# Two steps of a head group multiplied with the values as one job, and the planner's costs and due times rewritten

## The reference: one transformer block over 16 sequences

```python
mod = (silu(c) @ wmod).reshape(16, 6, 1, 256)           # sa, ca, ga, sb, cb, gb per sequence
ga, gb = (sign-keeping maximum of |g| and 0.25)
h = layernorm(x) * (1 + ca) + sa
Q, K, V = (h @ w.T + b), split into 16 heads of 16
scores = Q @ K^T / 4 + slope[head] * (k - q), causal    # [16, 16, 1024, 1024]
x = x + ga * (softmax(scores) @ V @ o_w.T + o_b)
h = layernorm(x) * (1 + cb) + sb
x = x + gb * ffn(h)          # silu(gate) * up, down; width 704; inputs and weights rounded
                             # to a 4-bit grid with one scale per 16 numbers (fp4_linear)
```

## Time and profile before

| what | before |
|---|---|
| median of 3 runs | 3672.09 us (3669.64 to 3675.01) |
| the profiled execution's own time | 3680.17 us |
| its span, first to last instruction | 3678.4 us |
| PE busy | 3400.2 us (92%) |
| DVE busy | 2859.7 us (78%) |
| ACT busy | 1862.1 us (51%) |
| POOL busy | 1082.0 us (29%) |
| granted TensorE clock, mean | 0.944 |

### The profile page before, as it was taken

The page is one execution under the profiler, slowest core; times in us unless marked ns, Lnnn a source line. Parts: engine busy times, 40 slices in busy tenths (PEclk is TensorE's granted clock), DMA queues, the critical chain, the costliest instruction groups (busy, mean ns, idle before and its releaser), DMA issues.

```text
span 3678.4 us, 62613 instructions
## 1 busy us (share of the span) xinstructions
PE 3400.2 (92%) x24952; PEld 1950.1 (53%) x24952; DVE 2859.7 (78%) x4538; ACT 1862.1 (51%) x2475; POOL 1082.0 (29%) x794
## 2 busy tenths in 40 slices
PE   6889999999999999999999999999999999999887
PEld 3345555555555555555555555555555555555455
DVE  7877869778786987868788786987868789687665
ACT  1555455555554555455555554655455555555441
POOL 2112324223242322324133142232323223241233
PEclk7889999999999999999998999999998999999898
DMA  8251413314323332423314323332423314332010
GB/s 152 55 81 28 76 40 68 65 28 77 56 53 60 52 70 39 79 44 61 65 32 72 56 50 63 51 68 42 79 48 56 66 33 71 57 50 54 16 32 12
DMA packets 134929, 207.65 MB, mean 56 GB/s; under 512 B 38848, under 2 KB 98832, under 8 KB 134640
## 3 DMA queue, kind: packets, MB, share of 16 engines
q1 hardware_dynamic: 134640, 203.66, 31.3%
HBM read 63.65 MB, written 17.89 MB: 22 GB/s over the span
## 4 chain that ended last, share of the span: by engine, by line
PE 71%; DVE 14%; ACT 10%; issue 2%; POOL 1%; DMA 1%; SPq 1%; ACTq 0%; POOLq 0%; DVEq 0%
PE banks L783 12%; PE banks L919 9%; PE banks L767 9%; ACT arena L982 8%; DVE top L1218 8%; PE banks L802 8%; PE banks L896 8%; PE banks L903 7%; PE banks L826 5%; PE banks L912 3%; PE banks L857 3%; PE banks L877 3%; PE banks L748 3%; ACT L982 2%; PE banks L887 1%
## 5 line engine op out<-in xcount | busy, mean ns | idle before, releaser
L1218 DVE TENSOR_REDUCE top<-banks 128x2 f32<-128x1024 f32 (+3 forms) x1280 | 1371.8, 1114 | 274.7 <-PE banks L748 171.4
L982 ACT ACTIVATE arena<-banks 128x1024 f32<-128x1024 f32 (+2 forms) x1280 | 1160.7, 940 | 784.4 <-PE banks L748 520.3
L802 PE MATMUL banks<-ka,qa 58*128 58x512 f32 (+3 forms) x3072 | 625.3, 442 | 130.1 <-ACT arena L982 94.2
L767 PE MATMUL banks<-qa,ka 60*128 60x512 f32 (+3 forms) x3072 | 590.9, 424 | 79.7 <-ACT arena L982 46.7
L783 PE MATMUL banks<-arena,va 128*17 128x512 f32 (+3 forms) x6144 | 641.1, 519 | 7.2 <-ACT arena L982 6.8
L767 PEld LDWEIGHTS banks<-qa,ka 60*128 60x128 f32 x3072 | 276.3, 192 | 407.2 <-ACT arena L982 175.2
L802 PEld LDWEIGHTS banks<-ka,qa 58*128 58x128 f32 x3072 | 291.1, 201 | 343.8 <-ACT arena L982 195.9
L1119 POOL TENSOR_TENSOR hid<-hid,tm 128x704 f32<-128x704 f32 x128 | 215.8, 1686 | 769.3 <-DVE hid L1196 769.3
L919 PE MATMUL banks<-wdT,hqT 128*128 128x256 f32 x1536 | 371.1, 392 | 3.4 <-ACT hqT L1024 3.4
L919 PEld LDWEIGHTS banks<-wdT,hqT 128*128 128x128 f32 x1536 | 290.1, 194 | 77.5 <-issue 23.1
L896 PE MATMUL banks<-wguT,xqT 128*128 128x352 f32 x1024 | 326.3, 462 | 0.7 <-ACT xqT L1015 0.7
(11 more groups left out here) (138 smaller groups left out, 4017.2 us busy)
## 6 DMA issues: line engine op xcount, KB each, us to landing
qa<-parts SPq DMA_DIRECT2D x384, 128.0 KB, 4.3
ka<-parts SPq DMA_DIRECT2D x384, 128.0 KB, 6.0
xa<-in_x SPq DMA_DIRECT2D x16, 1024.0 KB, 5.8
xr<-in_x SPq DMA_DIRECT2D x64, 256.0 KB, 3.0
out_x<-xr SPq DMA_DIRECT2D x64, 256.0 KB, 3.1
onT<-oT SPq DMA_DIRECT2D x252, 64.0 KB, 5.2
rsumT<-rsum_dram SPq DMA_DIRECT2D x63, 256.0 KB
ffn_rows<-rows_dram SPq DMA_DIRECT2D x16, 256.0 KB, 4.4
```

The lines of the kernel that those rows point to most:

```text
L767: mm = pe.matmul(ps[:, at:at + w], ka[g][rows, pair, kt * P:(kt + 1) * P], qa[g][rows, pair, q0:q0 + w], start=m == 0, stop=s not in DIAGO ...
L802: mm = pe.matmul(ps[:, at:at + w], qa[g][rows, pair, qt * P:(qt + 1) * P], ka[g][rows, pair, c * BANK:c * BANK + w], start=m == 0, stop=no ...
L982: nc.scalar.activation(heads.rearrange("p (m r) q -> p r m q", r=2), scores, ACT.Exp).then_inc(a_free, 1)
L1218: nc.vector.tensor_reduce(tops, scores, AX.X, ALU.max).then_inc(d_free, 1)
```

## The change

**One job for two steps.** PV jobs exist only for odd steps and multiply the slots of steps `s - 1` and `s`, one right after the other, with the same matmuls as before. The semaphore `pv_done` is then counted by pairs (`TURNS = 6` a group instead of 12), and ACT, before it overwrites a slot, waits for the pair that held it. The number of slots stays three.

**The planner's numbers.** Costs of ACT, DVE and POOL passes in `plan()` are replaced (most become smaller, a few larger), `SWITCH` goes from 0.09 to 0.095, and all the numbers of `SHIFT` are new, so the order differs nearly everywhere.

```diff
+TURNS = NS // 2
...
-    SHIFT = {"ACT CO": 62.0, "ACT GA": -91.0, "ACT HT": 37.0, "ACT LX": 48.0, "ACT T": 24.0, "ACT TR": -78.0, "ACT U": 13.0,
+    SHIFT = {"ACT CO": 164.0, "ACT GA": -153.0, "ACT HT": 106.0, "ACT LX": 22.0, "ACT T": 6.0, "ACT TR": -102.0,
...
-SWITCH = 0.09
+SWITCH = 0.095
...
-                   ring="D", on="DVE", takes_cost=0.16 + 1.042e-3 * w * 2 * n_pairs, banks=2,
+                   ring="D", on="DVE", takes_cost=0.135 + 1.042e-3 * w * 2 * n_pairs, banks=2,
...
-                       ("PE", ("PV", old // (NG * NS), old // NS % NG, old % NS)) if i == 0 else None, ring="A", on="ACT",
-                       takes_cost=0.17 + 0.833e-3 * w * heads, banks=2)
+                       ("PE", ("PV", old // (NG * NS), old // NS % NG, old % NS | 1)) if i == 0 else None, ring="A", on="ACT",
+                       takes_cost=0.125 + 0.833e-3 * w * heads, banks=2)
...
-                p.add("PE", ("PV", b, g, s), 1.9e-3 * w + 0.03, due + 3, ("ACT", ("T", b, g, s, jobs_of(s) - 1)),
-                      ("PE", ("PV", b, g, s - 1)) if s else None, ("ACT", ("V", b, 1)) if (g, s) == (0, 0) else None, lag=0.22,
-                      banks=1 if s in FIRST else 0, holder=("ACT", ("CO", b, g, c)) if s in FIRST else None)
+                if s % 2:
+                    first = s - 1 in FIRST
+                    p.add("PE", ("PV", b, g, s), 1.69e-3 * (w + span(s - 1)[1]) + 0.02, due + 3, ("ACT", ("T", b, g, s, jobs_of(s) - 1)),
+                          ("PE", ("PV", b, g, s - 2)) if s > 1 else None, ("ACT", ("V", b, 1)) if (g, s) == (0, 1) else None, lag=0.22,
+                          banks=1 if first else 0, holder=("ACT", ("CO", b, g, c)) if first else None)
...
-            p.add("DVE", ("XQ", b, r), 2.75, due + 4, ("DVE", ("XR", b, r)), ring="Q")
-            p.add("POOL", ("XQ", b, r), 2.6, due + 6, ("DVE", ("XQ", b, r)), takes="Q")
+            p.add("DVE", ("XQ", b, r), 3.2, due + 4, ("DVE", ("XR", b, r)), ring="Q")
+            p.add("POOL", ("XQ", b, r), 2.35, due + 6, ("DVE", ("XQ", b, r)), takes="Q")
...
                         pe.wait_ge(a_free, in_a["T", b, g, s, jobs_of(s) - 1])
-                        for h in range(G):
-                            mm = pe.matmul(out[32 * h:32 * h + VW, :], va[:, kt, g * G + h, :],
-                                           probs[:, s % P_SLOTS, h, 0:w], start=s in FIRST,
-                                           stop=s in LAST, skip_group_check=True)
+                        for step in (s - 1, s):
+                            kt, c = STEPS[step]
+                            q0, w = span(step)
+                            out = bank(("PV", b, g, FIRST[c] + 1))[:, q0 - c * BANK:q0 - c * BANK + w]
+                            for h in range(G):
+                                mm = pe.matmul(out[32 * h:32 * h + VW, :], va[:, kt, g * G + h, :],
+                                               probs[:, step % P_SLOTS, h, 0:w], start=step in FIRST,
+                                               stop=step in LAST, skip_group_check=True)
                         mm.then_inc(pv_done, 1)
...
-                        if j == 0 and (b * NG + g) * NS + s >= P_SLOTS:
-                            act.wait_ge(pv_done, (b * NG + g) * NS + (s - P_SLOTS + 1))
+                        old = (b * NG + g) * NS + s - P_SLOTS
+                        if j == 0 and old >= 0:
+                            act.wait_ge(pv_done, old // 2 + 1)
```

More of the change, by code:

```diff
@@ L334, in normalise @@
         if g % 2:
-            p.add("POOL", ("MUL", b, g // 2, *half), 2.4, due + 10.0, *(("SP", (k, b, g - 1)) for k in ("NUM", "RBC")),
+            p.add("POOL", ("MUL", b, g // 2, *half), 2.45, due + 10.0, *(("SP", (k, b, g - 1)) for k in ("NUM", "RBC")),
                   *(("SP", (k, b, g, *half)) for k in ("NUM", "RBC")), lag=8.0)
@@ L369, in feed_forward @@
             pe(("O", b, r), 1.75, at + 2.0 + r, ("POOL", ("MUL", b, 0)), ("POOL", ("MUL", b, 1, *half)), ("POOL", ("WG", b)),
-               ring="D", on="DVE", takes_cost=2.0, then=(("POOL", ("FOLD", b, r)), ("DVE", ("LN", b - 1, NPAIR - 1))))
+               ring="D", on="DVE", takes_cost=1.75, then=(("POOL", ("FOLD", b, r)), ("DVE", ("LN", b - 1, NPAIR - 1))))
         for half in (0, 1) if b == HALVED[0] else ((),):
             mine = range(NPAIR) if half == () else (2 * half, 2 * half + 1)
-            p.add("DVE", ("LR", b) if half == () else ("LR", b, half), 2.4, at + 6.0, *(("DVE", ("O", b, r)) for r in mine))
+            p.add("DVE", ("LR", b) if half == () else ("LR", b, half), 2.1, at + 6.0, *(("DVE", ("O", b, r)) for r in mine))
         first, every = at + 0.06 * L, 0.235 * L
@@ L391, in feed_forward @@
                        ("PE", ("GA", b, t, 0)) if k else (("PE", ("GA", b, t - 1, 1)) if t % 2 else None),
-                       ring="A", on="ACT", takes_cost=1.8 if 2 * (t % 2) + k in (0, 3) else 0.5,
+                       ring="A", on="ACT", takes_cost=1.75 if 2 * (t % 2) + k in (0, 3) else 0.46,
                        lock=((b, r), t % 2 == 1 and k == 1))
                 pe(("UP", b, t), 2.4, late + 2, ("PE", ("GA", b, t, 1)), ("PE", ("UP", *tile(t - 1))), ring="D", on="DVE",
-                   takes_cost=0.95, banks=2, then=(("ACT", ("GA", b, t, 1)),))
-                p.add("DVE", ("HR", b, t), 1.75, late + 4, ("DVE", ("UP", b, t)), ("DVE", ("HQ", *tile(t - 1))))
-                p.add("DVE", ("HQ", b, t), 3.15, late + 6, ("DVE", ("HR", b, t)), ring="Q")
-                p.add("POOL", ("HQ", b, t), 3.4, late + 8, ("DVE", ("HQ", b, t)), takes="Q")
+                   takes_cost=0.89, banks=2, then=(("ACT", ("GA", b, t, 1)),))
+                p.add("DVE", ("HR", b, t), 1.66, late + 4, ("DVE", ("UP", b, t)), ("DVE", ("HQ", *tile(t - 1))))
+                p.add("DVE", ("HQ", b, t), 2.9, late + 6, ("DVE", ("HR", b, t)), ring="Q")
+                p.add("POOL", ("HQ", b, t), 3.1, late + 8, ("DVE", ("HQ", b, t)), takes="Q")
                 for k in range(2):
@@ L403, in feed_forward @@
                 pe(("DN", b, t), 2.75, late + 14, ("ACT", ("HT", b, t, 1)), ("PE", ("DN", *tile(t - 1))), ring="D", on="DVE",
-                   takes_cost=0.47, then=(("POOL", ("RES", *tile(t - 2))), ("SP", ("FGATE", b))))
+                   takes_cost=0.43, then=(("POOL", ("RES", *tile(t - 2))), ("SP", ("FGATE", b))))
                 p.add("POOL", ("RES", b, t), 0.8, late + 16, ("DVE", ("DN", b, t)), ("POOL", ("RES", *tile(t - 1))))
@@ L773, in run @@
                         _, _, g, s = e
[L774 to L776 removed]
+                        if s - 1 in FIRST:
                             open_banks(e)
[L778 to L779 removed]
+                        if g == 0 and s == 1:
                             pe.wait_ge(a_free, in_a["V", b, 1])
                         pe.wait_ge(a_free, in_a["T", b, g, s, jobs_of(s) - 1])
[L782 to L785 removed]
+                        for step in (s - 1, s):
[6 more added lines that the diff above has]
+                                               stop=step in LAST, skip_group_check=True)
                         mm.then_inc(pv_done, 1)
@@ L948, in run @@
                             act.wait_ge(sums_in, 16 * n)
-                        nc.scalar.copy(oT[:, c * BANK:(c + 1) * BANK], bank(("PV", b, g, FIRST[c]))).then_inc(o_free, 1)
+                        nc.scalar.copy(oT[:, c * BANK:(c + 1) * BANK], bank(("PV", b, g, FIRST[c] + 1))).then_inc(o_free, 1)
                         continue
@@ L966, in run @@
                         if b:
-                            act.wait_ge(pv_done, b * NG * NS)
+                            act.wait_ge(pv_done, b * NG * TURNS)
                         act.wait_ge(a_full, full)
```

29 lines of the change are left out of this document (12 added, 17 removed), and 12 rows, old and new, of the table SHIFT.

## The result

The changed kernel is slower: 3749.62 us, median of 4 executions (3744.89 to 3755.38), where the kernel before, run beside it, took 3670.86 us (3658.59 to 3675.01). The ratio is 1.0221, 95% interval 1.0192 to 1.0250. The forecast of 3646 us was off by 104 us, and the time lies outside its range.

What follows compares the result with a forecast made beforehand. PE's list was taken to bound the kernel, with short hand-overs at the banks. Profiled 3680.2 us less 26.3 of split changes, waits at 0, gave 3653.9; the median 8.1 lower gave 3646, 8-in-10 range 3600 to 3684.

Steps and rivals of the forecast that it cites:

- the pairing by itself adds no wait there: PV's wait for exponentials on PE: PV jobs short of cover fall from 176 to 111, 41 to 19 us; gain counted nothing.
- the shuffled waits: Bank waits moved by the new order: valued at 0, bound 28 us either way, as two counts disagreed in sign.
- The count over all banks: PE work missing behind bank hand-overs: 508 us short before, 536 after; at a need of 2.2 us, 2280 and 2043.
- What it removes: Changes of array split on PE: 134 fewer PV stretches save 28.1 us, 20 more row-half changes cost 1.8; net 26.3.
- What it moves: Planner costs nearer the trace, unpriced; ACT, DVE and POOL work unchanged; TOP transfers nearer their use, hidden by about 1 us.
- TOP is in time: Transfer from `topT` ahead of T: hidden by about 1 us; the rival that it comes late, 3664 us, had chance 0.06.
- an order with fewer surprises: Planner costs of ACT and DVE passes nearer the trace speak for a better order; not priced, left in the range.
- The sum: Whole kernel: profiled 3680.2 us less 26.3 is 3653.9; the median 8.1 us lower gives 3646.
- The clock rivals: PE's granted clock: one fall less per batch, 3603 us, chance 0.15; one fall more, 3689 us, chance 0.12.
- What PE saves is waited away: PE's waits for ACT and DVE banks take back 6 us (3652) or all 26 us (3672); chance 0.15.
- The rival that ended on the slower side: Longer T and S stretches on PE cause one clock fall more in each of 14 batches: +43 us, 3689; chance 0.12.

Runs made afterwards that it cites:

- e3: Order of the kernel before, only each even PV step moved next to its odd partner on PE (286 moved down): 3804.33 us, ratio 1.0335.
- e9: e3 with the 286 moved steps also still multiplied at their old place: 3823.49 us, ratio 1.0429.
- e14: e3 with the 286 moved steps multiplied twice at the joined place: 3955.01 us, ratio 1.0787.
- e2: Kernel before with all the new costs and due times, single PV steps, order planned anew: 3704.23 us, ratio 1.0099.
- e1: Kernel before with paired steps, old costs, `SWITCH` and `SHIFT`, order planned anew: 3918.52 us, ratio 1.0671.
- e10: Kernel before with paired steps, new costs and `SWITCH`, old `SHIFT`, order planned anew: 3818.70 us, ratio 1.0418.
- e13: Changed kernel, pairs whole, plus copies of 256 first steps at the earlier places used in e4: 3881.98 us, ratio 1.0593 to the kernel before.
- e5: Kernel before, same order, with four slots instead of three at run time: 3668.38 us, ratio 1.0010.
- e8: Changed kernel with four slots that the planner knows of, order planned anew: 3703.55 us, ratio 1.0096 to the kernel before.
- e4: Changed kernel's order with the first step of four of each group's six pairs multiplied earlier, alone: 3845.21 us, ratio 1.0472 to the kernel before.
- e12: Kernel before, single steps and old numbers, with four slots that the planner knows of, order planned anew: 3877.12 us, ratio 1.0576.

## Why the prediction was wrong

**What failed: "the pairing by itself adds no wait there", and the 0, with a bound of 28 us, for the shuffled waits.** PE's idle time grew by 98.5 us. The step on the pairing was worked out for PV's own wait alone: how much PE work lies between an exponential and the PV job that reads it. For that wait it was right (7.2 to 1.1 us). It never asked what the even step did where it stood. A PV step of 512 columns is 0.98 us of PE work that, but for steps 0 and 4, asks no engine for a new bank, while an exponential takes 0.94 us and a pass of the maxima 1.11. It was the cover of the T and S jobs next to it. Joining two stretches saves 0.21 us once, and bares such a place. e3 shows the price with nothing else moved: 91 us more of idle time (278.2 to 369.6) for 286 moved steps, 0.32 us each, against some 26 us saved in all, since only 134 of these moves took a stretch away. e9 and e14 show that it is the place.

**How much of it is the changed kernel's.** The price of e3 can't be carried over whole. The new numbers without pairs (e2) already cost 68 us of the 98.5 of idle time and 36 us of time; pairs on top of them (the changed kernel against e2) add 31 us of idle time and 45 us of time. From the other side, pairs alone, planned anew with the old numbers (e1), cost 250 us, and the new numbers give 169 back. In idle time the two paths read 68 and 31 us, or 172 and -73. So no single split between the halves exists; but the shuffled order, which the forecast put at 0, brought waits of its own, well above the bound of 28 us.

**The count over all banks** (508 us short before, 536 after) was the right kind of count, and its sign was right at a need of 1.3 us. I gave it 0 because a second need turned the sign, and took its 28 us as a bound both ways. PE's idle time measured +98.5. A count that ranks two orders one way at one need and the other way at another bounds nothing.

**What it removes** held. PE busy fell by 23.2 us where 26.3 were forecast. Two steps of 512 columns take 1.84 us to the next job's start, in the median over the pairs of steps 4 with 5 and 6 with 7. There are 6144 records of PV.

**What it moves** held in the main: TOP is in time, for no row shows T waiting for the transfer from `topT` as a cause; ACT and DVE do as much as before. That planner costs nearer to the trace speak for "an order with fewer surprises" did not show: with single steps the new numbers as a whole cost 1.0% (e2), and only with pairs did the costs help (e10 against e1).

**The sum** against the profiled execution: -26.3 was -23.2 as measured, the waits 0 were +98.5; together +75.3, the whole change of the span.

**The rivals.** The clock rivals did not come in: 0.944 went to 0.946. "What PE saves is waited away" came nearest, a PE that waits longer for ACT and DVE: the waits grew, with ACT's and DVE's passes of unchanged length (0.94 us and 1.11 us, before and after). The Trainium skill (TensorEngine Tiling (Array Packing), PSUM Bottleneck) points there, saying that tiling speeds up TensorE and not the emptying of PSUM; the trace agrees in that PE's added idle time stands mostly ahead of jobs that need a bank. But I capped the rival at the saving, as if a bank wait could only eat what PE gains. In e3 the merge took more than it saved, since it also took away the work that hid the pass. The rival that ended on the slower side started from the same picture ("also gathers the T and S jobs between them") and priced it in falls of the clock; in the changed kernel the mean clock did not fall, and the price was in the waits themselves.

**What stays open.** Of the 98.5 us, 75 stand ahead of T. Work put at the parted places takes 66 of them back (e13), but how they divide between the pairs and the new numbers is not shown, for e2 has 66 of the 75 without pairs. Ahead of XT stand 37 more (3.5 to 40.5, 15.0 of it one single wait for POOL), and the `hid` pass has 17.4 ahead of S; these belong to the new order, and which of its numbers put them there was not separated. That a better tuned order of pairs could beat before is not excluded; none of the runs did. e5, which leaves the order alone, equals it, and the best with pairs is e8 at +1.0%. Parting the pairs of the changed kernel in place was tried once only (e4), at a clock so much lower (0.920) that it says little of the waits.

## What to carry to other kernels

Before merging two jobs to save a switch, ask of the one that moves not only whether its inputs are ready, but whose wait it was hiding where it stood: here such a step was worth 0.32 us of idle time between jobs that wait for banks, and a merge saved at most 0.21. Test a merge in the old order, by moving those jobs alone, before letting a planner lay out everything anew, for a replanned order can lose several per cent by itself (e12: 5.8% against 0.1%). When a change has two halves, read the waits of each half alone, not only its time: e2's 1.0% hid as large a wait ahead of T as the whole change has. And to tell a place from an amount, run the same extra work once at the old place and once at the new one.

## What was unexpected of the hardware

The granted clock moved with where PV's work stands, in ways that I could not foresee. Before it was 0.944. Joining steps in place gave 0.933 (e3), with 194 us more of PV at the old places 0.958 (e9), at the joined place 0.950 (e14); parting the changed kernel's pairs took it from 0.946 to 0.920 (e4), and copies at the same places, with the pairs kept whole, gave 0.950 (e13). More PE work went with a higher clock in e9, e14 and e13, and this paid for part of it. The same kernel also varies: e3's four executions lay at 0.933, 0.934, 0.939 and 0.947, and took 3814, 3813, 3795 and 3775 us. Here 0.014 of clock goes with 39 us, a half of the loss that the change itself brought. Why parting the pairs lowers it is not settled.

A second surprise is a stall whose total stays and whose place costs. In the batch of the changed kernel shown above, DVE stands still for 4.93 us at the head of its list, for sums that come by DMA behind the row transfers of the next batch. The timeline of SP and DVE:

```profile
1448.18 3.76 SPq L637 DMA_DIRECT2D qa<-parts  x6
1452.03 3.75 SPq L637 DMA_DIRECT2D ka<-parts  x6
1455.88 0.62 SPq L658 DMA_DIRECT2D sums<-oT  x1
...
1463.13 0.35 DVE L1246 RECIPROCAL rsums<-sums 128x32 f32<-128x32 f32 x1 [4.93 <-DMA sums<-oT]
```

SP's queue gives each of these issues about 0.63 us (3.76 for six), so the transfer of `sums` leaves 7.7 us after the first of them. It is a reason why SPq and DMA hold 3% each of the chain. DVE's waits of this kind sum to 67.7 us after (17 times) and 69.7 before (20 times), so the stall itself is not new. What is new is what comes behind it: in each of the 14 places where S waits for the `hid` pass (17.4 us in all), S starts 5.6 to 5.7 us after DVE comes out of such a stall, and before the change S has no wait for `hid`. SPq and DMA held 1% each of the chain before. These places come with the new numbers: e2, without pairs, has 7 of them, ahead of T.
